# A four-layer kernel on one core: products of zeros at the beginning, row sends and one head re-ordered, and ternary transposes moved between two groups of products

## The reference

```python
xn = _layernorm(x);  x = x + L0_attn(xn) + L0_ffn(xn)   # chunked linear attention, 16 heads; gated FFN with spline weights
xn = _layernorm(x);  x = x + L1_attn(xn) + L1_ffn(xn)   # window attention, 16 heads of 128, with rotary; 7 routed experts + 1 shared
xn = _layernorm(x);  x = x + L2_attn(xn) + L2_ffn(xn)   # gated scan (HGRN); product with binarized weights
xn = _layernorm(x);  x = x + L3_attn(xn) + L3_ffn(xn)   # complex linear recurrence; gated FFN with ternary weights
```

## Time and profile before

| | us |
|---|---|
| time, three runs | 687.96, 692.9, 690.5 (median 690.5) |
| the profiled execution's own time | 684.86 |
| its span, first to last instruction | 683.3 |
| mean granted TensorE clock in it | 0.995 |

### The profile page before, as it was taken

The page is one execution under the profiler, slowest core; times in us unless marked ns, Lnnn a source line. Parts: engine busy times, 40 slices in busy tenths (PEclk is TensorE's granted clock), DMA queues, the critical chain, the costliest instruction groups (busy, mean ns, idle before and its releaser), DMA issues.

```text
span 683.3 us, 13489 instructions
## 1 busy us (share of the span) xinstructions
PE 642.0 (94%) x4844; PEld 504.5 (74%) x4844; DVE 529.0 (77%) x1068; ACT 346.2 (51%) x752; POOL 335.5 (49%) x267
## 2 busy tenths in 40 slices
PE   3998999999899999999999999989989998899987
PEld 1445778788478988888898787878968746657766
DVE  4278876698698998988899998576437879689994
ACT  1497212300556485755647565465454663279441
POOL 1053555592457677474857736898238432120000
PEclk9999999999999999999999999999999999999999
DMA  8801000000601001010100102102321200100001
GB/s 250 347 1 63 2 2 1 1 1 0 239 17 40 25 8 38 19 42 16 38 23 8 38 16 57 46 22 61 139 68 44 58 1 0 39 0 1 1 1 62
DMA packets 14647, 31.37 MB, mean 46 GB/s; under 512 B 1837, under 2 KB 8587, under 8 KB 14029
## 3 DMA queue, kind: packets, MB, share of 16 engines
q1 hardware_dynamic: 12813, 26.46, 11.8%
q0 software_dynamic: 1536, 3.15, 1.8%
q10 hardware_dynamic: 256, 1.18, 0.6%
HBM read 26.59 MB, written 5.24 MB: 47 GB/s over the span
## 4 chain that ended last, share of the span: by engine, by line
PE 53%; DVE 17%; issue 11%; ACT 10%; POOL 4%; DMA 3%; SPq 0%; DVEq 0%; POOLq 0%; ACTq 0%
PE bank L613 9%; PE bank L614 7%; PE bank L615 7%; PE bank L603 6%; PE bank L594 6%; PE bank L806 3%; DVE arena L1740 2%; PE bank L836 2%; DVE arena L1739 2%; PE bank L820 2%; PE bank L835 2%; DMA arena<-in_lA 2%; DVE x L1765 2%; DVE arena L1749 1%; PE bank L709 1%
## 5 line engine op out<-in xcount | busy, mean ns | idle before, releaser
L613 PE MATMUL bank<-zone 128*128 128x256 f32 (+1 forms) x472 | 167.4, 355 | 11.2 <-DVE arena L1740 3.0
L614 PE MATMUL bank<-zone 128*128 128x256 f32 (+1 forms) x472 | 156.6, 332 | 0.0
L615 PE MATMUL bank<-zone 128*128 128x256 f32 (+1 forms) x472 | 156.4, 331 | 0.0
L613 PEld LDWEIGHTS bank<-zone 128*128 128x128 f32 x472 | 88.9, 188 | 36.8 <-issue 12.2
L2209 POOL TENSOR_TENSOR arena<-arena 128x512 f32<-128x512 f32 x64 | 82.2, 1284 | 61.2 <-ACT arena L1317 61.2
L615 PEld LDWEIGHTS bank<-zone 128*128 128x128 f32 x472 | 89.1, 189 | 9.1
L2214 POOL TENSOR_TENSOR arena<-arena 128x512 f32<-128x512 f32 x64 | 83.1, 1298 | 24.3 <-DVE arena L1740 13.6
L614 PEld LDWEIGHTS bank<-zone 128*128 128x128 f32 x472 | 89.2, 189 | 5.2
L1336 ACT ACTIVATE arena<-arena 128x256 f32<-128x256 f32 (+1 forms) x128 | 62.1, 487 | 29.4 <-DVE arena L1749 28.8
L1749 DVE CUSTOM_DVE_ANT_0 arena<-bank,const 128x256 f32<-128x256 f32 (+1 forms) x128 | 45.7, 403 | 23.6 <-PE bank L806 22.2
L1765 DVE SCALAR_TENSOR_TENSOR x<-bank,arena,x 128x256 f32<-128x256 f32 x128 | 53.0, 473 | 9.2 <-PE bank L615 8.5
(11 more groups left out here) (298 smaller groups left out, 1331.4 us busy)
## 6 DMA issues: line engine op xcount, KB each, us to landing
arena<-in_qk SPq DMA_DIRECT2D x16, 256.0 KB, 2.7
arena<-in_tern SPq DMA_DIRECT2D x1, 3072.0 KB, 22.4
arena<-in_wv SPq DMA_DIRECT2D x8, 256.0 KB, 2.9
arena<-in_wo SPq DMA_DIRECT2D x16, 128.0 KB, 2.1
arena<-in_wr SPq DMA_DIRECT2D x1, 1792.0 KB, 9.3
lB<-in_lB SPq DMA_DIRECT2D x1, 1288.5 KB, 24.9
x<-in_x SPq DMA_DIRECT2D x2, 512.0 KB, 8.0
xg_rows<-arena SPq DMA_DIRECT2D x1, 1024.0 KB
```

The costliest lines, as they stand in the source:

```text
L613: pe.matmul(dst, lhi, rhi, start=(n == 0), stop=False)
L614: pe.matmul(dst, lhi, rlo, start=False, stop=False)
L615: last = pe.matmul(dst, llo, rhi, start=False, stop=(n == len(terms) - 1 and not open_end))
```

## The change

- `x` tiles 0 to 3 come in two transfers of two tiles with a semaphore each; VectorE measures the first two tiles while the others arrive. `phase` moves from ScalarE's queue to SyncE's, behind the first part of `lA`.
- VectorE first clears one block of `xT`, and TensorE makes six products of 512 columns of these zeros into a bank that is overwritten later.
- The 16 row sends are placed anew: three in the middle of head 11 and four behind it, one in the middle of head 12 and six behind it, two in the middle of head 13. None stands ahead of `turn_qk` any more.
- In head 14, TensorE waits for two banks only, makes head 15's projections 0 and 1, and then waits for the other two and makes the scores.
- In layer 2 the 16 ternary transposes stand between the second and the third of the four groups of `g_ffn2`; one `stay_busy` product of 512 columns stands before the wait for `z2`. Bank numbers of these groups change with the order.

```diff
@@ build
-        g_ffn2 = groups(x_added, NT // 2)
+        g_ffn2 = groups(x_added, 2)
         g_wT3 += groups(wT3_ready, TERN // (8 * P) - len(g_wT3))
+        g_ffn2 += groups(x_added, NT // 2 - 2)
@@ sync
-            sp.dma_start(x[:, 0:TPB, :], dram["x"][:, 0:TPB, :]).then_inc(x_loaded, 16)
+            sp.dma_start(x[:, 0:2, :], dram["x"][:, 0:2, :]).then_inc(x_loaded, 16)
+            sp.dma_start(x[:, 2:TPB, :], dram["x"][:, 2:TPB, :]).then_inc(x_second, 16)
             sp.dma_start(x[:, TPB:NT, :], dram["x"][:, TPB:NT, :]).then_inc(x_rest, 16)
             sp.dma_start(lA[:, 0:A_V], dram["lA"][:, 0:A_V]).then_inc(lA_loaded, 16)
+            sp.dma_start(phase[0:SPH, :], dram["phase"]).then_inc(spline_loaded, 16)
@@ tensor
+            pe.wait_ge(xT_clear, 1)
+            for _ in range(WARM):
+                pe.matmul(g_raw0[0][0].ps, xT[:, 0, 0:P], xT[:, 0, 0:BW], start=True, stop=True)
             pe.wait_ge(const_loaded, 16)
@@ head
                 if more:
                     project_qk(h + 1, 0, next_pair)
+                if score_left:
+                    project_qk(h + 1, 1, next_pair)
+                    for left in score_left:
+                        pe.wait_ge(*left)
                 scores(h, [2])
-                if more:
+                if more and not score_left:
                     project_qk(h + 1, 1, next_pair)
@@ tensor, head 14
-            for left in HEAD1["left"][0:4]:
+            for left in HEAD1["left"][0:2]:
                 pe.wait_ge(*left)
-            head(H1 // 2 - 1, 0, True, True, HEAD1, beside=shared_out)
+            head(H1 // 2 - 1, 0, True, True, HEAD1, beside=shared_out, score_left=HEAD1["left"][2:4])
@@ tensor, layer 2
             for p in range(NT // 2):
+                if p == 2:
+                    turn_ternary(range(4, len(g_wT3)))
                 tall(g_ffn2[p], p, lambda t: [(xT[:, k, tok(t)], bwT[:, k, :]) for k in range(KD)])
-            turn_ternary(range(4, len(g_wT3)))
...
+            stay_busy(g_wo2[0], BW, 1)
             pe.wait_ge(z2_ready, KD)
@@ vector
+            dve.memset(xT[:, 0, 0:BW], 0.0).then_inc(xT_clear, 1)
             dve.wait_ge(x_loaded, 16)
-            measure(range(TPB))
+            measure(range(2))
+            dve.wait_ge(x_second, 16)
+            measure(range(2, TPB))
@@ gpsimd
-            SENDS = {SPLIT - 3: (range(0, 3), range(3, 5)), SPLIT - 2: (range(5, 8), range(8, 10)), SPLIT - 1: (range(10, 14), range(14, 16))}
+            SENDS = {SPLIT - 3: (range(0, 3), range(3, 7)), SPLIT - 2: (range(7, 8), range(8, 14)), SPLIT - 1: (range(14, 16), ())}
             for h in range(SPLIT - 4, SPLIT):
...
-                send_rows(early)
-                beside_head(h, between=lambda: send_rows(later))
+                beside_head(h, between=send_between)
                 rest_of_wqk(h + 2)
                 if h % 2 == 0:
                     rest_of_wv(h // 2 + 1)
+                send_rows(behind)
```

## The result

| | before | after |
|---|---|---|
| median of the runs, us | 690.79 (687.96 to 692.9, 8 runs) | 696.21 (695.13 to 700.19, 8 runs) |
| ratio, 95% interval | | 1.0087 (1.0069 to 1.0106) |
| profiled execution, us | 684.86, span 683.3 | 700.19, span 698.4 |

The change costs 5.4 us by the medians, 0.8%, and 6.0 us (4.8 to 7.3) by the ratio; the forecast was 693 us, a plus of 2.75. The profiled executions lie far apart, 15.3 us: that of before is faster than all eight runs beside which it stands, that of after is the slowest of its eight. So their difference overstates the change, and what only one of them shows may belong to that execution. Lines have moved: the split products are L618 to L620 now, the scores L814, `turn_probs` L828, row maxima L1765, the sends L2253, GpSimd's rests L2187.

A forecast was written before the change was run, and what follows sets the result against it. TensorE, 53% of the chain, was taken as the bound, with only its idle and slow spots worth something. Terms -0.7 + 0 + 1.1 + 1.3 + 1.05 = +2.75 us gave 693.2 against the median of 690.5; range 685 to 698.

The forecast's parts named there:

- The beginning: Kernel start: statistics and all behind them 0.70 us earlier through the split x load; term -0.7, between 0 and -0.7.
- two statistics are done by then: Kernel start: when x tiles 2 and 3 land near 6.4, two of four statistics are done, so 0.70 us remain.
- The zeros: Kernel start: six zero products end near 6.5, TensorE idles at least 3 us, the clock is low again; term 0.
- The row sends: Heads 11 to 13, GpSimd: one send more ahead of w2s, 1.31 us less 0.3; term +1.1, bounds -1.9 to +1.3.
- against the profiled execution's own 684.86 us: The baseline on which the terms were made part by part; their sum was then also added to the runs' median, 690.5.
- the forecast's other number, 687.6: Whole kernel: the sum +2.75 us against the profiled 684.86 us, beside 693.2 against the median of the runs.
- Head 14: Head 14: additions to x 0.5 us earlier, clock fall behind a new 3.65 us gap costs 1.8; term +1.3.
- Layer 2: Layer 2: the 16 transposes delay the last group and z2 by 1.06 us; term +1.05, between -0.6 and +1.05.
- I expect the fall as before: Layer 2, output products: the clock falls ahead of them as before; if the fall is gone, 1.7 us is saved.
- The zeros keep the clock high: Rival at the kernel start: the six zero products hold the high clock, 3.0 us less, 690.2; chance 0.15.
- GpSimd isn't the bound: Rival at the row sends: they give -1.6 us (the wait at 459.98) instead of +1.1, 690.5; chance 0.15.
- Slower by more: Rival: clock falls behind TensorE's new 2.1 us wait at 473.6, 1.7 more, 695, up to 698; chance 0.13.

The follow-up runs named there:

- the beginning alone: The zero products, the split of x and the moved load of phase, on the kernel before: ratio 0.9988 (0.9969 to 1.0007), 689.32 beside 689.45.
- the second run of after: The whole change again on another chip, against the kernel before: ratio 1.0024 (1.0007 to 1.0040), 686.95 beside 685.17 us.
- The filled gap: The beginning with eight zero products and one product of constants, against the kernel before: ratio 0.9962, -2.6 us; the 16 wide products took 7.11 us.
- the chip of the four parts: Chip where beginning, row sends, head 14 and layer 2 each ran alone on the kernel before: ratios 0.9988, 1.0052, 1.0013 and 1.0014.
- the second run of the sends alone: The re-placed row sends on the kernel before, run again on a chip without late counts: ratio 1.0011 (0.9994 to 1.0027), 685.89 beside 685.36.
- the sends alone: Only the re-placed row sends, on the kernel before: ratio 1.0052 (1.0033 to 1.0072), 693.4 beside 689.45 us.
- the filling: Head 14's edit plus three products of constants in its new gap, against the kernel before: ratio 0.9981 (0.9965 to 0.9997), -1.3 us.
- the sends alone again: The re-placed row sends on the kernel before, a second time, on a chip without late counts: ratio 1.0011 (0.9994 to 1.0027), 685.89 us.
- layer 2 alone: Ternary transposes between the binary products and one stay_busy product, on the kernel before: ratio 1.0014 (0.9992 to 1.0036), +1.0 us.
- the cut row: Re-placed sends with the row of six cut to three and four, against the kernel before: ratio 1.0001, and 1.0013 when run again.
- the row without transfers: Re-placed sends with sends 8 to 13 replaced by six GpSimd multiplications, against the kernel before: ratio 1.0019 (0.9999 to 1.0039), +1.3 us.

## Why the prediction was right or wrong

The time lay in the range and the direction of the whole was right, but the plus was about twice the forecast, and for a reason that the forecast did not have. That 696.2 still lay in the range of 685 to 698 is in part luck: on a chip without late counts the change costs 1.6 us, so more than half of the plus is in something that no term stood for. Of the four parts only the sends, on the chip with the late counts, can be told from nothing by their time; the others rest on what the traces show.

**The beginning: -0.7 forecast, about nothing found.** The step that failed is "two statistics are done by then". The first two tiles landed no earlier than four did before, and VectorE took all four statistics from 6.36 on. The zeros came out as forecast, but not by the forecast's sum: it took 0.88 us for a product at the low clock, which is what one of its two instructions takes. So the six end at 8.4 us and not near 6.5, and the idle time behind them is 1.76 us, where at least 3 were forecast. The clock fell all the same: behind 1.76, 1.91 (the beginning alone) and 1.31 us (the second run of after, where it fell later and the 16 took 8.72 us). That was luck as far as the argument went, which rested on the gap being longer than 1.99 us. The filled gap has since shown the cause.

**The row sends: +1.1 forecast.** Where no count comes late, +0.8 and both waits of TensorE as told: 0.87 to 0.90 at the start of head 13, 1.75 at the output projection (2.1 forecast). `w2s` is issued at 482.10 in the second run of the sends alone, beside 481.19 when the rest ends at 481.16 in before: +0.9. On the chip of the four parts the sends cost 3.6. The 2.5 us more go with the late counts, a term that the sum lacked; that these waits make up the whole difference was not shown by taking them away there. Nothing in the trace of before shows the term, since that execution has none. The step that failed is to add terms made "against the profiled execution's own 684.86 us" to the median of other runs. The 5.6 us between that time and the median of 690.5 were a sign that these runs lose time somewhere where this trace does not. The profiled time is that of the chips without late counts (685.2 to 685.4), and there the forecast's other number, 687.6, stands beside a measured 686.95.

**Head 14: +1.3 forecast, +0.9 found.** The earlier additions won 0.5 us in all three traces with the edit and without the filling. The gap was 3.1 to 3.4 us (3.65 forecast), and the low clock behind it lasted 6.8 us in all three traces that have it, where 3.4 to 4.9 were forecast. In the changed kernel's second trace, which no late count disturbs, row maxima at 518.71 stand 2.39 behind before and the additions at 513.17 stand 1.38 behind: 1.0 us lost at once, and by 523.88 ScalarE's drain stands 3.6 behind its place of before (520.26), so 2.2 in all, beside 1.8 taken. The row on which the forecast leaned says less than it seemed to: the gap of 2.0 us of the old order is in seven traces, and a fall came close behind it in three of them (before, the sends alone again, layer 2 alone); behind the gap of 3.1 to 3.4 us it came in all three.

**Layer 2: +1.05 forecast, +1.0 found.** The stretch is 0.94 to 0.95 longer in every trace with the change. The clock is less settled. Without the edit the output products ran at the low clock in eight of eleven traces (8.68 to 8.86 us) and at the high clock in three (7.17). With it they ran low in one of three, that of after. So the fall differs from one execution to another, by up to 1.7 us, and the forecast "I expect the fall as before" held in one trace of three. Whether the product of `stay_busy` makes the fall rarer is open: three traces are too few.

**The rivals.** "The zeros keep the clock high" falls for six products, and holds when two more and one of constants are added. "GpSimd isn't the bound" falls by the 1.75 us wait, and by the time: its -1.6 lies outside the -0.4 to +1.9 of the sends where no count is late. "Slower by more" had the right size, 695 to 698, and a wrong mechanism in part: the clock did fall at head 13 (472.28), but behind a wait of 4.44 us that late counts made, not behind the 2.1 us wait for GpSimd; in the second run, with a gap of 1.75 us, it did not.

On a chip without late counts the forecast of +2.75 stands beside +1.6 (0.5 to 2.7), at the upper end of the interval or just outside it. The profiled spans of before and of the second run of after, neither with late counts, 683.3 and 686.2, differ by 2.9.

## What to carry to other kernels

A warm-up of TensorE is worth what is left of it when the real products start: fill the time up to them, or expect little of it. Work moved ahead of a wait moves the gap; measure the place where it comes out, and fill it where nothing else can stand there. Before a sum made on one profiled execution is set against a median, ask whether that execution is like the runs; here 5.6 us between the two was larger than the effect.

## What the hardware showed unexpectedly

In the profile of after and in all four of the chip of the four parts, the counts that TensorE adds to its semaphores arrived late beside rows of GpSimd's indirect transfers. In the trace of after three waits of VectorE are of this kind, 11.8 us together: 3.05 us behind a row of four sends (at 446.14), 5.22 behind the row of six, and 3.50 behind five fetches (at 541.78). Behind each of the last two the granted clock falls, at 472.28 and 543.96. The kernel before takes 685.2 to 685.4 us on three chips where no trace has it, and 689.5 to 690.8 where the traces of the kernels beside it do; no trace of the kernel before itself shows it. The changed kernel takes 686.95 and 696.2, the sends alone 685.9 and 693.4, so the re-placed sends make the kernel more exposed to it. The Trainium skill ("Perfetto Trace Analysis", section "Tensor Engine Instruction (MATMUL, LD_WEIGHTS)") says that a product's recorded end is computed and that its semaphore update and the propagation come after it, outside the record. The traces agree: in the timeline such a delay shows only as the idle time of whoever waits, put down to "remote".

What stays open: why this happened on some chips and not on others (the record does not name the chip of the first comparison), whether sends, fetches or their landings cause it, and whether shorter rows would help there, since the cut row and the row without transfers were only run on chips without it. That the waits end with the row speaks for shorter rows there, but is no test. That the longest wait stands behind the longest row is seen in two traces (5.22 and 5.04 us) and was not tried on its own there.
